# Maxima over the partitions of the weights: transpose, row maximum and diagonal product in place of GpSimd's instruction

## The reference

```python
def block(x, ctx, pad_mask, sub_mask, g_xattn, g_ffn, ...):
    # cross-attention: 16 heads of 32, 128 keys
    q = layernorm(x) @ Wq.T + bq;  k = ctx @ Wk.T + bk;  v = ctx @ Wv.T + bv
    att = q k^T / sqrt(32), -1e9 where pad_mask == 0 or sub_mask == 0
    x = x + tanh(g_xattn) * (softmax(att) @ v)
    # experts: 8 of width 256, the best two of each token, and a shared one of width 512
    h = layernorm(x)
    p = softmax(h @ router);  the two largest p of a token are its weights
    routed = sum over its two experts of p_e * (silu(h @ gate_e) * (h @ up_e)) @ down_e
    shared = (silu(h @ s_gate) * (h @ s_up)) @ s_down
    return x + tanh(g_ffn) * (routed + shared)
```

## Time and profile before

| | |
|---|---|
| time, median of 3 runs | 1175.54 us (1173.56 to 1176.14) |
| the profiled execution: span from the first to the last instruction | 1178.0 us |
| TensorE busy | 1047.6 us, 89% |
| VectorE busy | 821.4 us, 70% |
| ScalarE busy | 530.6 us, 45% |
| GpSimd busy | 442.5 us, 38% |
| mean granted TensorE clock | 0.942 |

### The profile page before, as it was taken

How to read it: one execution, slowest core, us unless ns; L and a number is a source line. 1 busy time by engine, 2 the same in 40 slices (tenths; PEclk the granted TensorE clock), 3 DMA queues, 4 the chain that set the end, 5 groups by cost and what they waited for, 6 DMA issues and landing times.

```text
span 1178.0 us, 26603 instructions
## 1 busy us (share of the span) xinstructions
PE 1047.6 (89%) x7335; PEld 673.1 (57%) x7336; DVE 821.4 (70%) x2932; ACT 530.6 (45%) x1041; POOL 442.5 (38%) x655
## 2 busy tenths in 40 slices
PE   5499858999999999870599999999999999999997
PEld 3377747777777787760255555555554444444443
DVE  3899856887888888875276666666665566666666
ACT  1266526666666666651244444444443222223232
POOL 1345526676666666643212222121210332222322
PEclk9699978998999899985699999999999999999999
DMA  5564572334333223422333333333342544545443
GB/s 194 216 224 164 129 181 75 92 91 91 91 103 95 88 97 91 108 95 32 98 118 108 121 111 121 111 118 114 117 124 73 161 158 154 173 142 174 150 162 125
DMA packets 76731, 146.96 MB, mean 125 GB/s; under 512 B 20912, under 2 KB 23088, under 8 KB 73872
## 3 DMA queue, kind: packets, MB, share of 16 engines
q1 hardware_dynamic: 46512, 66.01, 21.1%
q10 hardware_dynamic: 17280, 44.83, 10.6%
q0 software_dynamic: 12896, 35.58, 9.8%
HBM read 94.04 MB, written 52.35 MB: 124 GB/s over the span
## 4 chain that ended last, share of the span: by engine, by line
PE 59%; issue 14%; DVE 10%; POOL 8%; ACT 4%; DMA 2%; POOLq 1%; another core or an unknown queue 1%; DVEq 0%; ACTq 0%; SPq 0%
PE bank L1036 14%; PE bank L1037 14%; PE bank L1038 14%; PE bank L1028 8%; PE bank L1071 4%; DVE arena L768 3%; PE bank L1089 3%; POOL arena L466 2%; POOL token_of_row L502 2%; DVE arena L857 1%; ACT arena L612 1%; DMA token_of_row<-arena 1%; DVE peak L871 1%; PE bank L1102 1%; PE bank L1103 1%
## 5 line engine op out<-in xcount | busy, mean ns | idle before, releaser
L1028 PE MATMUL bank<-ident,arena 128*128 128x128 f32 (+1 forms) x1592 | 188.4, 266 | 89.6 <-DMA arena<-normed_rows,arena 30.0
L1036 PE MATMUL bank<-weights,arena 128*128 (+1 forms) x682 | 260.2, 382 | 2.1 <-ACT arena L654 1.9
L1037 PE MATMUL bank<-weights,arena 128*128 (+1 forms) x682 | 260.2, 381 | 0.0
L1038 PE MATMUL bank<-weights,arena 128*128 (+1 forms) x682 | 259.8, 381 | 0.0
L1028 PEld LDWEIGHTS bank<-ident,arena 128*128 128x128 f32 (+1 forms) x1592 | 160.4, 132 | 137.1 <-issue 100.3
L518 POOL DMA_INDIRECT arena<-normed_rows,arena x71 | 67.4, 949 | 241.8 <-PE bank L1028 227.0
L1089 PEld LDWEIGHTS bank<-arena 128*128 128x128 f32 x1024 | 128.6, 195 | 36.2 <-issue 27.7
L1071 PE MATMUL bank<-arena 128*128 128x512 f32 x256 | 140.4, 654 | 8.5 <-DVE arena L768 6.8
L466 POOL TENSOR_TENSOR arena<-arena 128x512 f32<-128x512 f32 x96 | 101.7, 1060 | 85.0 <-DVE arena L768 73.7
L768 DVE CUSTOM_DVE_ANT_0 arena<-bank,arena 128x128 f32<-128x128 f32 x512 | 116.8, 283 | 17.8 <-PE bank L1071 14.5
L1089 PE MATMUL bank<-arena 128*128 128x33 f32 x1024 | 125.7, 273 | 3.8 <-ACT arena L568 3.8
(11 more groups left out here) (170 smaller groups left out, 1890.5 us busy)
## 6 DMA issues: line engine op xcount, KB each, us to landing
expert_rows<-arena ACTq DMA_DIRECT2D x71, 256.0 KB, 2.1
arena<-in_x SPq DMA_DIRECT2D x64, 256.0 KB, 3.8
weights<-in_w_gu ACTq DMA_DIRECT2D x8, 1024.0 KB, 4.9
x_rows<-arena SPq DMA_DIRECT2D x32, 256.0 KB
normed_rows<-arena SPq DMA_DIRECT2D x32, 256.0 KB, 5.5
normed_transposed<-arena SPq DMA_DIRECT2D x32, 256.0 KB, 2.6
arena<-normed_transposed SPq DMA_DIRECT2D x32, 256.0 KB, 3.2
arena<-x_rows SPq DMA_DIRECT2D x32, 256.0 KB, 3.5
```

Source lines behind the costliest of these rows:

```text
L1028: last = t.transpose(dst[:, c * P:(c + 1) * P], src[:, c * P:(c + 1) * P], (ident16 if src.dtype == F16 else ident)[:, :])
L1036: t.matmul(dst, hi[:, rows], w_hi(c), start=(c == 0), stop=False)
L1037: t.matmul(dst, hi[:, rows], w_lo(c), start=False, stop=False)
L1038: last = t.matmul(dst, lo[:, rows], w_hi(c), start=False, stop=(c == chunks - 1))
```

## The change

The maximum over the partitions is now formed by TensorE and VectorE. `peak` becomes a 128x128 tile that is zeroed at first, so that TensorE can transpose it: column c of it becomes row c. VectorE takes the maximum of each row (`peak_top`, one value in partition c), multiplies the identity by it (`peak_diag`, the values on the diagonal), and TensorE multiplies a matrix of ones by that: each partition then holds all 128 maxima along its row of a PSUM bank. `scale_of` reads its column there. Each of the three uses is a `turn_peaks(bank, k)` on TensorE and a `spread_peaks(bank, k)` on VectorE. GpSimd's three instructions go, and it gets two more memsets at the start. The semaphores of the second loads of the down weights are merged into those of the first.

```diff
@@ GpSimd
+            g.memset(ones_f[:, :], 1.0).then_inc(pool_set, 1)
+            g.memset(peak[:, :], 0.0).then_inc(pool_set, 1)
...
-            pool.wait_ge(peak_set, 1)
-            g.partition_all_reduce(peak_all[:, 0:5:4], peak[:, 0:20:19], P, RMAX).then_inc(scale_set, 1)
...
-            def beside(it):
-                if it == CHUNKS:
-                    pool.wait_ge(peak_set, 2)
-                    g.partition_all_reduce(peak_all[:, 1:3], peak[:, 16:18], P, RMAX).then_inc(scale_set, 1)
...
-                if it == 2:
-                    pool.wait_ge(peak_set, 3)
-                    g.partition_all_reduce(peak_all[:, 3:4], peak[:, 18:19], P, RMAX).then_inc(scale_set, 1)
@@ VectorE
+            def spread_peaks(b, k):
+
+                dve.wait_ge(peak_moved, 2 * k - 1)
+                d.tensor_reduce(peak_top[:, :], bank[b][:, 0:P], AX.X, ALU.max).then_inc(scale_step, 1)
+                scales[0] += 1
+                dve.wait_ge(scale_step, scales[0])
+                d.tensor_scalar(peak_diag[:, :], ident[:, :], peak_top[:, :], None, ALU.mult).then_inc(diag_ready, 1)
+                dve.wait_ge(peak_moved, 2 * k)
...
+            spread_peaks(6, 1)
+            scale_of(0, 6, 0)
+            scale_of(4, 6, 19)
...
-                if it == HEAD1 - 1:
-                    scale_of(1, 6)
-                    scale_of(2, 8)
+                if it == SPREAD_IT:
+                    spread_peaks(0, 2)
+                    scale_of(1, 0, 16)
+                    scale_of(2, 0, 17)
...
-                if it == 3:
-                    scale_of(3, 11)
+                if it == 2:
+                    spread_peaks(4, 3)
+                    scale_of(3, 4, 18)
@@ TensorE
+            def turn_peaks(b, k):
+                pe.wait_ge(peak_set, k)
+                t.transpose(bank[b][:, 0:P], peak[:, :], ident[:, :]).then_inc(peak_moved, 1)
+                pe.wait_ge(diag_ready, k)
+                t.matmul(bank[b][:, 256:256 + P], ones_f[:, :], peak_diag[:, :], start=True, stop=True).then_inc(peak_moved, 1)
+
+            pe.wait_ge(const_set, 1)
+            pe.wait_ge(pool_set, 6)
+            turn_peaks(6, 1)
...
+            def beside(it):
+                if it == SPREAD_IT:
+                    pe.wait_ge(q_ready, it - 1)
+                    turn_peaks(0, 2)
+                    pe.wait_ge(scale_set, 4)
...
             def beside2(it):
+                if it == 2:
+                    turn_peaks(4, 3)
```

More of the change, by code:

```diff
@@ L22 @@
 AX = mybir.AxisListType
-RMAX = bass.bass_isa.ReduceOp.max
 P = 128
@@ L109, in build @@
         half_power = sb("half_power", [P, 1])
-        peak = sb("peak", [P, 20])
-        peak_all = sb("peak_all", [P, 5])
+        peak = sb("peak", [P, P])
+        peak_top = sb("peak_top", [P, 1])
+        peak_diag = sb("peak_diag", [P, P])
+        ones_f = sb("ones_f", [P, P])
         w_scale = sb("w_scale", [P, 5])
@@ L234, in build @@
         chunk_in = sems(" ".join(f"chunk_in{i}" for i in range(ALL_CHUNKS)))
-        again_in = sems(" ".join(f"again_in{i}" for i in range(DOWN_CHUNKS)))
         x_here, res_here, xn2_out, x2t_out, x1_out, rows_out = (
@@ L327, in build @@
         SPLIT_J = HEAD1 // 2
+        SPREAD_IT = HEAD1 - 1
         def split_beside(it):
@@ L625, in beside @@
                     for i in range(CHUNKS, ALL_CHUNKS - 1):
-                        act.dma_start(raw(i), chunk_src(i)).then_inc(again_in[i - CHUNKS], 16)
+                        act.dma_start(raw(i), chunk_src(i)).then_inc(chunk_in[i], 16)
                 if it == HEAD1 - 1:
-                    act.wait_ge(scale_set, 10)
+                    act.wait_ge(scale_set, 4)
                 for i in split_beside(it):
@@ L633, in down_high @@
                 act.wait_ge(prep_lo, i + 1)
-                act.wait_ge(again_in[i - CHUNKS], 16)
+                act.wait_ge(chunk_in[i], 32)
                 a.activation(down_halves(i)[0], by_expert(down_raw(i)), ACT.Copy, scale=w_scale[:, 2:3]).then_inc(prep_hi, 1)
@@ L697, in beside2 @@
                 if it == 4:
-                    act.wait_ge(scale_set, 13)
+                    act.wait_ge(scale_set, 5)
                     a.activation(swd[:, 0, :], swd_raw, ACT.Copy, scale=w_scale[:, 3:4]).then_inc(prep_hi, 1)
@@ L712, in _ @@
             d.memset(kbd, 0.0).then_inc(kv_set, 1)
+            dve.wait_ge(pool_set, 6)
             d.memset(vaug[:, :, :, D:D + 1], 1.0)
@@ L717, in _, with scale_of @@
             d.tensor_reduce(peak[:, 19:20], router_s[:, :, :].rearrange("p c n -> p (c n)"), AX.X, ALU.max, apply_absolute_value=True).then_inc(peak_set, 1)
-            scales = [0]
-            def scale_of(i, at):
-                dve.wait_ge(scale_set, at)
-                d.tensor_scalar(w_back[:, i:i + 1], peak_all[:, i:i + 1], TINY, None, ALU.max).then_inc(scale_set, 1)
-                dve.wait_ge(scale_set, at + 1)
+            scales, scaled = [0], [0]
+            SPREAD_AT = 256
+            def spread_peaks(b, k):
[5 more added lines that the diff above has]
+                dve.wait_ge(peak_moved, 2 * k)
+            def scale_of(i, b, col):
+                d.tensor_scalar(w_back[:, i:i + 1], bank[b][:, SPREAD_AT + col:SPREAD_AT + col + 1], TINY, None, ALU.max).then_inc(scale_step, 1)
+                scales[0] += 1
+                dve.wait_ge(scale_step, scales[0])
                 bits = w_back[:, i:i + 1].bitcast(I32)
@@ L727, in scale_of @@
                 scales[0] += 1
-                dve.wait_ge(scale_step, 2 * scales[0] - 1)
+                dve.wait_ge(scale_step, scales[0])
                 d.reciprocal(w_scale[:, i:i + 1], w_back[:, i:i + 1]).then_inc(scale_step, 1)
-                dve.wait_ge(scale_step, 2 * scales[0])
+                scales[0] += 1
+                dve.wait_ge(scale_step, scales[0])
                 back = 1.0 / W_TOP if i in (2, 3) else 1.0 / (W_TOP * X_SCALE)
@@ L733, in scale_of @@
                 d.tensor_scalar(w_scale[:, i:i + 1], w_scale[:, i:i + 1], W_TOP, None, ALU.mult).then_inc(scale_set, 1)
-                dve.wait_ge(scale_set, at + 2)
-            scale_of(0, 1)
-            scale_of(4, 3)
+                scaled[0] += 1
+                dve.wait_ge(scale_set, scaled[0])
+            spread_peaks(6, 1)
+            scale_of(0, 6, 0)
+            scale_of(4, 6, 19)
             dve.wait_ge(router_hi, 1)
```

16 lines of the change are left out of this document (8 added, 8 removed).

## The result

The changed kernel takes 1156.33 us (median of 4 runs, 1154.43 to 1157.58); the kernel before, beside it on that chip, 1175.84 us (4 runs, 1173.56 to 1177.84). The ratio is 0.9831, 95% interval 0.9809 to 0.9852: 19.5 us faster, where 20.9 were forecast. Measured again on another chip it took 1161.55 us (6 runs) against 1175.19 us: 0.9881, 0.9848 to 0.9914, which is 13.6 us. Both medians lie in the forecast range of 1146 to 1165.

What follows compares the result with a forecast made beforehand. TensorE's work sets the pace except in three holes: the start, step 11 (GpSimd's code swaps) and between the passes. Gains 7.5 + 12.7 + 0.7 = 20.9 us, from 1175.5 to 1154.6 us; range 1146 to 1165.

Steps and rivals of the forecast that it cites:

- the start: Start of the kernel up to pass 1 on TensorE: exchange replaces GpSimd's reduction, 7.5 us gained, from 3 to 9.3.
- Rival 2: At the start, TensorE's new place in the queue eats what VectorE wins, so nothing is gained: 1162.1 us; chance 0.06.
- Step 11: Step 11 of pass 1: 18.4 us removed, less 3.2 and 2.5, a gain of 12.7 us, from 11.8 to 15.2.
- the stop and both swaps: Step 11: TensorE's 15.84 us stop and GpSimd's code swaps around the reduction go; with the slower clock, 18.4 us.
- the exchange, 3.2 us: End of step 11: TensorE's uncovered exchange, 1.5 us, plus VectorE's two scales, 1.7 us, cost 3.2 us.
- Rival 3: Step 11: a wait like ScalarE's 5.90 us one in step 10 comes into the open: 1163.9 us; chance 0.10.
- The clock's share: After the nearly idle exchange at step 11's end, TensorE falls to half clock, losing 2.5 us.
- the other branch of rival 3: Step 10: ScalarE's 5.90 us wait is not there at the new timing: 1145.3 us; chance 0.07.
- the three signs of being wrong: Exchange costs several microseconds more than its rows, step 11 keeps a wait for GpSimd, or step 10's wait moves.
- Pass 2: Pass 2: TensorE's exchange replaces the reduction that delayed GpSimd's gather of slot 3; gain 0.7 us, from -1 to 1.
- Rival 1: Step 11: only 5.80 us of each GpSimd wait belongs to the reduction, the rest stays: 1162.0 us; chance 0.05.
- Rival 4: Pass 2: shared weights' maximum comes late and TensorE stands with everything behind it; slower, 1184 us if at 610; chance 0.03.

## Why the prediction was right, and where it was off

*What bounds the kernel, and the start.* Right: forecast 7.5 us, the start of step 3 came 7.4 us earlier (42.72 instead of 50.08). Each intermediate time is within 1 us: exchange over at 16.0 (15.9), the values' products from 24.9 (24.7), pass 1 at 34.5 (34.1). Rival 2 fell. The early identity, which I had not foreseen, gives nothing here, as the kernel with the exchange only at the start shows (6.2 us with the identity late).

*Step 11.* The step that was off. Forecast: 18.4 removed, 3.2 for exchange and scales, 2.5 for the clock, net 12.7. Measured: the stop and both swaps did go, and step 11 is 11.5 us shorter (31.1 to 19.6); behind it the clock costs 1.5 us of step 12; net 10.0. The term that was mis-sized is "the exchange, 3.2 us": it is 6.9. Of the 3.7 us more, 0.4 to 1.1 are an error of the sizes (exchange and scales take 3.6 to 4.3 us where no hole is in them; the product, put at 0.45 us, takes up to 0.80 at half clock), and about 3 are VectorE's hole, TensorE's late signals. Rival 3 named such a wait, at 0.10 and 9.3 us, and it came at a third of that. Its account was wrong in two points: the wait in step 10 does have a semaphore in the kernel, TensorE's `xt_done`, raised late; and that the 19 us stop had hidden such a wait isn't shown, for in the kernel before no signal of TensorE in step 11 is late by 1 us. The clock's share was put 1.0 us too high. "In step 10 ScalarE stood for 5.90 us" came as 3.71, and step 11 starts 9.3 us earlier where the start alone gave 7.4: 2.0 us that make up for most of the hole. They belong to the other branch of rival 3. Nothing in the change asks for them, and the kernel with one unread reduction has 5.76 there, so this is luck. Of the three signs of being wrong two came: the exchange costs several microseconds more than its rows, and the wait of step 10 changed.

*Pass 2.* Forecast 0.7 us. From the shared weights' maximum to the last output there are 596.7 us instead of 597.5, which is 0.7. TensorE's waits of 1.08 and 2.41 us are those forecast. What the forecast missed is that taking this reduction away moves the next execution's start, worth 5 us where the first reduction is kept.

*Rival 1* was right about a piece: 4.8 of the 19.0 us of waits go when the transfers beside them go. It was wrong about what follows, since that piece goes with the swap as well. *Rival 4* fell: the maximum came at 555.81 + 2.27 = 558.1 us, and no load was waited for.

Sum of what the trace shows at step 12's end (181.83 instead of 201.13): 19.3 us; at the end of the span 22.2. Of the difference 0.7 is pass 2's, and 2.2 us come in the rest of pass 1, where no term of the forecast lies; in the second execution that stretch loses 2.0 us instead. By the medians the gain is 19.5 and 13.6. The forecast of 20.9 lies between span and medians; that it comes so near is in part luck (the 2.0 us of step 10 and these 2.2), and the second measurement says that it is on the high side.

## What to carry to other kernels

An instruction that needs GpSimd to change its loaded code should be priced by the idle rows before and behind it, not by its own 0.4 us: here a pair of waits of 14.2 us in the middle of a program, and of 19 to 25 us with transfers beside it. It is paid whether or not the result is read: one unread reduction in the middle gave the whole gain back. One that stands last is paid at the start of the next execution. When a long stop is removed, other waits of some 3 us can stand in its place, and the operations put in place of it belong ahead of where their result is needed: that was worth another 9 us by the traces and 14.6 by the medians.

## What the runs showed that was not expected

- A state of GpSimd outlasts an execution: 11 us of idleness before the first identity instruction in the four kernels that end with GpSimd's code as the last reduction left it (11.02, 11.29, 11.49, 11.53 us), and 0.36 us in the four that have a reduction but not as the last of its kind.
- The wait before one and the same reduction was 6.61 to 17.81 us, and shortest without the 3 MB load beside it.
- The waits of VectorE and ScalarE that the profile calls "remote" end with semaphores of TensorE that went up 2 to 5 us behind the recorded end of its instructions, where half of its signals come within 0.02 us.
- A stop of 0.57 us left TensorE at its higher clock, 2.4 GHz (12 transposes in 1.52 us). With step 11's exchange hidden it stood for 2.7 of the 3.0 us before 163.10 and came out at 1.2 GHz (2.82 us). But the same stop of 2.6 us at the start of pass 1 left it at the higher clock in one execution of the changed kernel (4 transposes in 0.63 us) and not in the other (1.09 us).
- Two executions of one program differ by 4.8 us of span, all of it in pass 1, and the median of the changed kernel was 1156.3 us on one chip and 1161.6 us on another, while the kernel before stayed within 1175 to 1180.
